# Two-stage gated feed-forward kernel: the output normalisation moved from ScalarE to VectorE

## What is computed

```python
x = L0_attn_x                       # 4 x 512 x 512, float32: 2048 rows of 512
x = x + _layernorm(_L0_attn_ref(_layernorm(x), w_gate, w_up, w_down))
x = x + _layernorm(_L0_ffn_ref(_layernorm(x), W_gate, W_up, W_down))

# _L0_attn_ref:  s = silu(x @ w_gate.T)       (1376 wide)
#                the 688 entries of smallest |s| in each row are set to 0
#                return (s * (x @ w_up.T)) @ w_down.T
# _L0_ffn_ref:   return (silu(x @ W_gate.T) * (x @ W_up.T)) @ W_down.T
# _layernorm:    (y - mean(y)) / sqrt(var(y) + 1e-5), over the last axis
```

## Time and profile before

| what | us |
|---|---|
| three runs, median (lowest to highest) | 786.13 (786.05 to 786.14) |
| the profiled execution, its own time | 787.0 |
| its span, first to last instruction | 785.0 |
| TensorE busy in the span | 766.9 (98%) |
| VectorE busy | 406.5 (52%) |
| ScalarE busy | 346.5 (44%) |
| GpSimd busy | 117.8 (15%) |

### The profile page before, as it was taken

How to read it: one execution, slowest core, us unless ns; L and a number is a source line. 1 busy time by engine, 2 the same in 40 slices (tenths; PEclk the granted TensorE clock), 3 DMA queues, 4 the chain that set the end, 5 groups by cost and what they waited for, 6 DMA issues and landing times.

```text
span 785.0 us, 9833 instructions
## 1 busy us (share of the span) xinstructions
PE 766.9 (98%) x3593; PEld 646.2 (82%) x3593; DVE 406.5 (52%) x822; ACT 346.5 (44%) x575; POOL 117.8 (15%) x278
## 2 busy tenths in 40 slices
PE   8999999999999999999989999999999999999996
PEld 7888888888888888889877788788878888788884
DVE  7686766766667666785783443253224332151114
ACT  6787665656656666566843221131112111131112
POOL 0533321122211222212310000010001000010001
PEclk9999999999999999999999999999999999999999
DMA  8520102222022220223713101020010210021001
GB/s 288 165 74 28 45 32 77 77 77 76 2 77 77 76 91 28 77 78 103 276 43 137 59 15 40 1 94 15 13 41 28 67 41 1 0 93 42 0 1 54
DMA packets 22338, 51.18 MB, mean 65 GB/s; under 512 B 2320, under 2 KB 5904, under 8 KB 22096
## 3 DMA queue, kind: packets, MB, share of 16 engines
q1 hardware_dynamic: 22288, 50.54, 19.3%
HBM read 42.14 MB, written 16.84 MB: 75 GB/s over the span
## 4 chain that ended last, share of the span: by engine, by line
PE 83%; DVE 7%; ACT 3%; issue 3%; POOL 2%; DMA 1%; DVEq 0%; POOLq 0%; SPq 0%; ACTq 0%
PE gu_ps L468 29%; PE gu_ps L418 23%; PE y_ps L447 13%; PE tr_ps L489 11%; PE y_ps L489 4%; PE tr_ps L432 2%; ACT junk L617 1%; PE tr_ps L400 1%; DMA xin<-in_L_attn_x 1%; PE gu_ps L400 1%; DVE below L973 1%; POOL thr L1224 1%; POOL move L1221 1%; DVE gate_lo L846 1%; DVE up_lo L858 0%
## 5 line engine op out<-in xcount | busy, mean ns | idle before, releaser
L617 ACT ACTIVATE junk<-absv,thr 128x1383 bf16<-128x1383 f32 x96 | 139.3, 1451 | 57.9 <-POOL thr L1224 56.4
L1023 DVE TENSOR_TENSOR prod<-gu_ps,prod 128x512 f32<-128x512 f32 (+1 forms) x44 | 30.4, 690 | 182.9 <-PE gu_ps L468 182.9
L418 PE MATMUL gu_ps<-up_hi,xT 128*128 128x460 f32 (+1 forms) x384 | 111.3, 371 | 0.0
L418 PE MATMUL gu_ps<-gate_hi,xT 128*128 128x460 f32 (+1 forms) x384 | 111.1, 370 | 0.0
L447 PE MATMUL y_ps<-down_hi,hT 128*128 128x512 f32 (+1 forms) x352 | 110.3, 395 | 0.0
L673 ACT ACTIVATE prod<-gu_ps 128x512 f32<-128x512 f32 (+1 forms) x44 | 26.3, 597 | 127.4 <-PE gu_ps L468 127.4
L447 PEld LDWEIGHTS y_ps<-down_hi,hT 128*128 128x128 f32 (+1 forms) x352 | 66.9, 190 | 15.0
L418 PEld LDWEIGHTS gu_ps<-gate_hi,xT 128*128 128x128 f32 x384 | 72.2, 188 | 7.8
L418 PEld LDWEIGHTS gu_ps<-up_hi,xT 128*128 128x128 f32 x384 | 72.2, 188 | 7.7
L447 PE MATMUL y_ps<-down_lo,hT 128*128 128x512 f32 (+1 forms) x176 | 70.3, 399 | 4.5 <-DVE hT L892 4.4
L418 PE MATMUL gu_ps<-up_lo,xT 128*128 128x460 f32 (+1 forms) x192 | 73.2, 381 | 1.5 <-DVE up_lo L846 0.8
(11 more groups left out here) (115 smaller groups left out, 1370.3 us busy)
## 6 DMA issues: line engine op xcount, KB each, us to landing
xin<-x_scratch SPq DMA_DIRECT2D x18, 256.0 KB, 3.2
xin<-in_L_attn_x SPq DMA_DIRECT2D x16, 256.0 KB, 4.6
xres<-in_L_attn_x SPq DMA_DIRECT2D x16, 256.0 KB, 4.8
x_scratch<-xres SPq DMA_DIRECT2D x16, 256.0 KB, 2.0
xres<-x_scratch SPq DMA_DIRECT2D x14, 256.0 KB, 2.8
out<-xres SPq DMA_DIRECT2D x14, 256.0 KB, 2.1
raw<-in_L_ffn_W_gate SPq DMA_DIRECT2D x4, 688.0 KB, 4.9
raw<-in_L_ffn_W_up SPq DMA_DIRECT2D x4, 688.0 KB, 4.7
```

The lines of the kernel that those rows point to most:

```text
L418: last = nc.tensor.matmul(dst[:, 0:CW[n]], xt, w, start=(c == 0 and i == 0), stop=(c == KC - 1 and i == 2))
L617: nc.scalar.activation(junk[:, 0:I + PAD], absv[:, q, 0:I + PAD], ACT.Sign, bias=thr[:, q:q + 1], scale=-1.0, accum_out=sgn[:, q:q + 1]).t ...
L1023: nc.vector.tensor_tensor(prod[0:k, 0, GW:2 * GW], bank(("u", idx, 0))[0:k, :], prod[0:k, 0, 0:GW], ALU.mult).then_inc(p2_done, 1)
```

## The change

The ScalarE pass and the bias go away. VectorE subtracts the mean in the PSUM bank right behind the statistics (`centre_y`, new), while GpSimd computes `yrstd` alone; `add_residual` then becomes one `scalar_tensor_tensor`: bank times `yrstd` plus residual. The last tile is still done in two halves, now straight from the bank. GpSimd's reuse of a column of `yrstd` waits on `res_done` instead of `ynorm_done`.

```diff
-            def normalise_y(b):
-                act.wait_ge(yb_done, b + 1)
...
+            def centre_y(b):
+
+                q = b % 4
+                nc.vector.tensor_scalar(y_bank(b)[:, :], y_bank(b)[:, :], ymv[:, q, 0:1], None,
+                                        ALU.subtract).then_inc(ycentred, 1)
+
             def add_residual(b):
+                q = b % 4
...
+                dve.wait_ge(yr_done, b + 1)
+                dve.wait_ge(ycentred, b + 1)
                 if b == XT2 - 1:
                     for i in range(2):
                         cols = slice(i * HALF, (i + 1) * HALF)
-                        dve.wait_ge(ynorm_done, b + i + 1)
-                        nc.vector.tensor_tensor(res_buf(b)[:, cols], ylast[:, cols], res_buf(b)[:, cols],
-                                                ALU.add).then_inc(half_done, 1)
+                        nc.vector.scalar_tensor_tensor(
+                            res_buf(b)[:, cols], y_bank(b)[:, cols], yrstd[:, q:q + 1], res_buf(b)[:, cols],
+                            ALU.mult, ALU.add).then_inc(half_done, 1)
                     return
-                dve.wait_ge(ynorm_done, b + 1)
-                nc.vector.tensor_tensor(res_buf(b), y_bank(b)[:, :], res_buf(b), ALU.add).then_inc(res_done, 1)
+                nc.vector.scalar_tensor_tensor(res_buf(b), y_bank(b)[:, :], yrstd[:, q:q + 1], res_buf(b),
+                                               ALU.mult, ALU.add).then_inc(res_done, 1)
...
                 if b >= 4:
-                    pool.wait_ge(ynorm_done, b - 3)
+                    pool.wait_ge(res_done, b - 3)
                 nc.gpsimd.tensor_tensor(yrstd[:, q:q + 1], yvar[:, q:q + 1], half[:, :], ALU.pow).then_inc(yr_done, 1)
-                pool.wait_ge(yr_done, b + 1)
-                nc.gpsimd.tensor_scalar(ybias[:, q:q + 1], ymv[:, q, 0:1], yrstd[:, q:q + 1], -1.0,
-                                        ALU.mult, ALU.mult).then_inc(yb_done, 1)
```

More of the change, by code:

```diff
@@ L125, in sandwich @@
         yrstd = sb("yrstd", [P, 4])
-        ybias = sb("ybias", [P, 4])
         half = sb("half", [P, 1])
@@ L175, in y_bank @@
             return (tr_ps[0], tr_ps[1], tr_ps[2], y_ps)[b % GT]
-        ylast = junk[:, 0:2 * H].bitcast(F32)
         def res_buf(b):
@@ L193, in sandwich @@
         s2_done, p2_done, h2hi_done, h2lo_done = map(sem, ("s2_done", "p2_done", "h2hi_done", "h2lo_done"))
-        silu_done, xhi_done, hhi_done, ynorm_done, counted = map(
-            sem, ("silu_done", "xhi_done", "hhi_done", "ynorm_done", "counted"))
+        silu_done, xhi_done, hhi_done, ycentred, counted = map(
+            sem, ("silu_done", "xhi_done", "hhi_done", "ycentred", "counted"))
         a_done, p_done, xn_done, xlo_done, hlo_done, res_done = map(
@@ L201, in sandwich @@
                   "any_done", "h_done"))
-        xr_done, yr_done, yb_done, thr_done, pool_step = map(
-            sem, ("xr_done", "yr_done", "yb_done", "thr_done", "pool_step"))
+        xr_done, yr_done, thr_done, pool_step = map(
+            sem, ("xr_done", "yr_done", "thr_done", "pool_step"))
         guess_done, unit_done, step_done = map(sem, ("guess_done", "unit_done", "step_done"))
@@ L737, in _ @@
             count(2, 2)
-            normalise_y(0)
             count(2, 3)
@@ L759, in _ @@
                 count(j, 3)
-                normalise_y(j - 2)
                 count(j, 4)
@@ L778, in _ @@
             count(last, 4)
-            normalise_y(last - 2)
             split_pair_hi(NPAIR + 1)
@@ L788, in _ @@
             split_pair_hi(NPAIR + 3)
-            normalise_y(last - 1)
             silu2(1)
@@ L802, in _ @@
                         silu2(idx)
[L803 to L807, removed]
                     if idx == 3:
@@ L810, in _ @@
                     split_h2_hi(idx)
-                    if g > 0 and j == 0:
-                        normalise_y(TILES + GT * (g - 1))
-                        normalise_y(TILES + GT * (g - 1) + 1)
                     if g == 0 and 3 <= j < 3 + NPAIR - 1:
@@ L817, in _ @@
                         split_x_hi(TILES + GT * (g + 1) + X_AT[j])
-            for r in range(GT):
-                normalise_y(XT2 - GT + r)
         @block.vector
@@ L1080, in _ @@
             y_stats(0)
+            centre_y(0)
             select(1)
@@ L1099, in _ @@
                 y_stats(j - 2)
+                centre_y(j - 2)
                 times_up(j, 0)
@@ L1120, in _ @@
             y_stats(last - 2)
+            centre_y(last - 2)
             split_pair_lo(NPAIR + 1)
@@ L1132, in _ @@
             y_stats(last - 1)
+            centre_y(last - 1)
             split_pair_lo(3)
@@ L1149, in _ @@
                         y_stats(last)
+                        centre_y(last)
                     times_up2(idx)
@@ L1156, in _ @@
                             y_stats(b + r)
+                            centre_y(b + r)
                         add_residual(b)
@@ L1173, in _ @@
                 y_stats(XT2 - GT + r)
+                centre_y(XT2 - GT + r)
                 if r:
```

## The result

The changed kernel takes 788.57 us (median of 9 runs, 787.86 to 788.82), the kernel before, run beside it, 786.14 (9 runs, 785.65 to 788.11). The ratio is 1.0025, with a 95% interval of 1.0015 to 1.0036: slower, by 2.4 us. The profiled execution took 788.57, its span is 786.8; of before, 787.0 and 785.0. So the medians are 2.4 apart, the two profiles only 1.6 to 1.8.

The account below looks back on a forecast made before the run. TensorE, busy 98% of the span, was taken as the bound, so VectorE's work costs only where TensorE waits. -3.2 + 4.3 + 0.9 = +2.0 us on the median run's 786.13 gave 788.0; range 784.4 to 790.2, the forecast's own 787 to 789.

Parts of the forecast that it names:

- Durations: VectorE's new `centre_y` and new `add_residual` take 0.75 us each; each pass pushes what follows by 0.67.
- Rival 2: VectorE's centring runs at SBUF's rate, 0.49 us, a push of 0.41: -1.5 us, or 784.6; chance 0.08.
- First half: nothing: Tiles 0 to 12: no change, since VectorE comes out no later and TensorE's products cover all of it.
- Where the halves meet, the chain: Tiles 13 to 15: TensorE starts at 393.4 in place of 394.5, then at 412.2 in place of 413.86: -1.6.
- Rival 4: GpSimd's threshold step slips in ahead of VectorE's weight pair: 1.0 us more gained in the middle, 787.1; chance 0.16.
- Where the halves meet, the clock: In `down` of tile 15, TensorE's clock stays up because both idle stretches are shorter: another -1.6 us.
- Boundaries: +4.3: Second half's group boundaries: later additions delay store, load and x tile, costing +1.7, +2.4 and 0.2 us.
- Rival 3: Boundaries are covered, so TensorE waits less: half paid gives 785.9, none 783.8; chance 0.14, three quarters of it faster.
- The end: +0.9: After the last product VectorE is the chain and waits for nothing; the last halves end at 783.5: +0.9 us.
- Rival 1: TensorE's clock falls again, behind idle stretches at 411 or at a boundary: 1.6 us for one fall, 789.7; chance 0.22.

Follow-up runs that it names:

- the first mixed kernel: The changed kernel, but tiles 16 to 27 (the three group boundaries of the second half) normalised by ScalarE as before: 784.76 us, ratio to before 0.9977.

## Why the prediction was right, and where it wasn't

The forecast was 788.0, slower, and 788.57 came, within the forecast's own range. By its steps:

- **Durations.** `centre_y` 750 ns for 0.75, the new addition 744 for 0.75, the push 0.67 (two centrings, at 775.78 and 777.45, lie 1.67 apart, of which 1.0 is the next bank's statistics). Rival 2, SBUF's rate, is out. So the Trainium skill's rule (VectorE: DVE Perf Modes, "Why PSUM operands drop a tier") agrees with this trace: with a PSUM operand the pass did not run at the rate of the 546 ns row.
- **First half: nothing.** Measured -0.34. In the two profiles this was hidden behind a start that came 0.61 later. The step was right that no later work of VectorE costs anything there, and put at nothing a gain that it didn't look for.
- **Where the halves meet, the chain.** Predicted 393.4 and 412.2, measured 393.70 and 412.45, of which 0.26 is the delay from before this place. The stretched threshold step came as read from the earlier trace rows, 388.49 to 389.85 where 388.2 to 389.55 was forecast, and moving it ahead took the stretch away. Rival 4 (it slips in ahead of the pair's low part) didn't happen by itself: here the pair was 0.03 us ahead. As for the Trainium skill's rule there (SBUF — State Buffer, "Who interferes with whom", whoever issues first keeps the interface), the trace agrees where VectorE is first: GpSimd's step, 0.03 us behind, took 1.36 in place of 0.29. No run here shows GpSimd first and VectorE held up.
- **Where the halves meet, the clock: the step that failed.** "With both stretches shorter I take the clock to stay up: another -1.6" is true of the profile of before and not of its median run. The prediction turned one execution's fall into a saving of every execution, although it had noted that this execution stood 0.9 above the median run. Two more executions of before show the fall costing nothing, or not there. Of 60 timed runs of before in all, 15 took over 787; which course their clock took isn't recorded, but the median ones have no 1.6 to give back. That the clock stays up in the changed kernel was right, and it is worth nothing there. By medians the first half and this place together are worth -2.3 (the first mixed kernel is 1.4 below before and pays 0.9 at its end), and not -3.2. The parts are 0.3 in the first half, 1.7 in the chain (1.1, and 18.75 from `down` of tile 14 to that of 15 in place of 19.33), nothing by the clock, and 0.2 outside the span (a run is 2.0 us longer than its span in before, 1.8 in the changed kernels).
- **Boundaries: +4.3.** Measured +3.8 in the profiles and 3.8 and 4.0 by undoing and by doing them alone. The first was right (1.7), the second too dear (2.4, measured 1.6), the third too cheap (0.2, measured 0.5). At the second, the forecast's shift of 2.8 for the x tile kept the old distance from the store to the load, 2.86 us. With the change the distance is 2.10, the value of the first boundary, since the pair of store issues takes 1.00 and not 1.74. SP's timeline in before, in its last profiled execution, and in after:

```profile
604.76 1.74 SPq L292 DMA_DIRECT2D out<-xres  x2
607.62 0.94 SPq L307 DMA_DIRECT2D xres<-x_scratch  x2
```
```profile
603.42 1.59 SPq L292 DMA_DIRECT2D out<-xres  x2
```
```profile
606.11 1.00 SPq L289 DMA_DIRECT2D out<-xres  x2
608.21 0.98 SPq L304 DMA_DIRECT2D xres<-x_scratch  x2
```

The slow issues are no accident of one execution. At this boundary they take 1.35 to 1.86 us in all seven profiles in which ScalarE normalises the banks (1.74, 1.51 and 1.59 in before), and 0.99 to 1.00 in all six in which VectorE does. So the change takes 0.8 us off that path; what makes the issues slow isn't shown. At the third, one wait for `res_done` was counted, and the trace has two (0.42 and 0.40 on the weight loads). Rival 3, covered boundaries, is out: at the first, the DMA wait grew from 1.21 to 2.14 instead of closing up.
- **The end: +0.9.** Measured +0.9, with VectorE never idle. Its own list gives 0.7 of that, and the other 0.2 passes between the end of the last half and the end of the span (2.5 us in place of 2.3), which the forecast took as unchanged.
- **Against the median.** -0.3 (first half) - 1.7 (chain) - 0.2 (outside the span) + 3.8 + 0.9 = +2.5, measured 2.4. The forecast's -3.2 + 4.3 + 0.9 came to +2.0. That it lies so close is in part luck: a clock gain of 1.6 that the median doesn't have was mostly made up for by boundaries 0.5 too dear, by the 0.3 and the 0.2 that it left out, and by 0.1 on the chain. Rival 1, a second fall of the clock, didn't happen: after, with stretches of 1.2 and 1.5, has none in its profile.

## What to carry to other kernels

A pass that moves to an engine with idle time costs by its place in that engine's list: ask which store, load or product stands behind it, and put the pass behind the first result that frees a buffer. Here the same 32 passes cost 2.8 us less once two of the four at each boundary stood behind the first two additions and the next step's product. And before counting something in a profile as what a change can give back, or as fixed, look whether a second execution of the same kernel has it. Here the clock's fall was not in every execution of before, while the slow pair of store issues was in all three. To compare two profiles, measure distances from an event behind the start: the start alone scattered by 0.6 us in before and hid a gain of 0.34.

## What the runs showed of the hardware that was not expected

With the same idle stretches of 2.3 and 2.1 us, TensorE's granted clock fell behind the second (0.82 over 9.25 us), behind the first (0.78 over 7.7 us) or behind neither, in three executions of one program; with a stretch of 2.07 made on purpose it fell in the profiled run (0.81 over 9.1 us) and, by the times, in one of five others. And a fall right behind a stretch is free when another engine's chain sets the next one: the second stretch shrank from 2.08 to 0.42. The issues of two stores of 256 KB on SP took 1.35 to 1.86 us at one boundary in seven profiles, and 0.99 to 1.00 in the six whose stores came behind VectorE's own passes. A GpSimd operation on 128x1 took 0.29 us alone and 1.36 when it began 0.03 us behind a VectorE operation of 1.23 with two SBUF inputs.
